# A five-stage layer on one Trainium2 core: the last image's scores on six banks, clears and queue instructions moved between engines

## The reference

```python
x = x + L0_conv_ref(gn(x))        # group norm, then a two-dimensional LSTM over rows and columns:
#   f0 = sigmoid(pf0 + h_up @ uf0), f1 = sigmoid(pf1 + h_left @ uf1), i, o, c~ from h_up + h_left
#   c = f0 * c_up + f1 * c_left + i * c~;  h = o * tanh(c)
t = tokens(x)                     # (16, 4096, 128)
t = t + L1_attn_ref(ln(t))        # Nystroem attention, 8 heads of 16, 64 landmarks:
#   q_l, k_l = means over 64 tokens
#   out = softmax(q k_l) @ pinv(softmax(q_l k_l)) @ (softmax(q_l k) @ v) + conv33(v)
t = t + L1_ffn_ref(ln(t))         # Wx = x W', batch-normalised; then 4096 steps in order:
#   y = sigmoid(Wx[:, t] + y @ V.T)
```

## Time and profile before

| | |
|---|---|
| median of 3 runs | 5966.88 us (5963.65 to 5968.33) |
| the profiled execution | 5969.65 us |
| its span | 5967.9 us |
| PE busy | 5291.5 us (89%) |
| ACT, DVE, POOL busy | 3264.5, 2989.0, 1673.9 us |
| mean granted clock of PE | 0.978 of 2.4 GHz |
| group norm / LSTM begins / landmark begins / recurrence begins | 0 / 221.4 / 1446.6 / 3660.3 us |

### The profile page before, as it was taken

The page is one execution under the profiler, slowest core; times in us unless marked ns, Lnnn a source line. Parts: engine busy times, 40 slices in busy tenths (PEclk is TensorE's granted clock), DMA queues, the critical chain, the costliest instruction groups (busy, mean ns, idle before and its releaser), DMA issues. The chain is left out here.

```text
span 5967.9 us, 208944 instructions
## 1 busy us (share of the span) xinstructions
PE 5291.5 (89%) x90032; PEld 3235.7 (54%) x90032; DVE 2989.0 (50%) x7682; ACT 3264.5 (55%) x9359; POOL 1673.9 (28%) x2017
## 2 busy tenths in 40 slices
PE   5599999997899997799999997888888888888888
PEld 4599888996566666644444443333333333333333
DVE  8677777775888885568888884000000000000000
ACT  5465555564677775479999994333333333333333
POOL 2100000002888874257877783000000000000000
PEclk7799999999999999999999998999999999999999
DMA  9631112225888772368777773111111111111111
GB/s 389 263 114 58 57 58 70 73 86 180 245 246 243 238 229 90 101 177 230 228 227 231 227 211 104 42 49 47 45 49 47 45 49 47 45 49 47 46 48 31
DMA packets 858992, 755.53 MB, mean 127 GB/s; under 512 B 71152, under 2 KB 732656, under 8 KB 854000
## 3 DMA queue, kind: packets, MB, share of 16 engines
q1 hardware_dynamic: 841120, 642.58, 36.1%
q0 software_dynamic: 14816, 99.32, 4.1%
q10 hardware_dynamic: 2160, 0.66, 0.0%
HBM read 425.72 MB, written 308.45 MB: 123 GB/s over the span
## 5 line engine op out<-in xcount | busy, mean ns | idle before, releaser
L2652 ACT ACTIVATE f_y<-f_acc 128x16 f32<-128x16 f32 x4096 | 753.7, 184 | 1544.0 <-PE f_acc L2618 1544.0
L2618 PEld LDWEIGHTS f_acc<-f_y,f_vT 128*32 128x32 f32 x32768 | 645.0, 108 | 1491.2 <-ACT f_y L2652 1491.2
L2618 PE MATMUL f_acc<-f_y,f_vT 128*32 128x16 f32 x32768 | 1045.8, 193 | 296.3 <-ACT f_y L2652 0.4
L2607 PE MATMUL f_junk<-f_idle 128*32 128x512 bf16 x12368 | 1226.0, 377 | 0.0
L2563 DVE TENSOR_TENSOR f_sum<-f_turned,f_t 128x512 f32<-128x512 f32 x128 | 88.5, 692 | 2072.3 <-PE f_turned L2600 2072.2
L2317 DVE TENSOR_REDUCE o_m<-o_bank_l 128x8 bf16<-128x512 f32 x512 | 327.3, 680 | 101.2 <-PE o_bank_l L2083 101.2
L2607 PEld LDWEIGHTS f_junk<-f_idle 128*32 128x32 bf16 x12368 | 368.0, 99 | 0.0
L1239 ACT ACTIVATE a_p<-a_s 128x512 f32<-128x512 f32 x512 | 264.2, 602 | 180.7 <-PE a_s L1111 180.6
L498 POOL DMA_DIRECT2D hidden<-l_h x46 | 34.6, 754 | 1160.2 <-DVE l_hsum L754 961.5
L677 ACT ACTIVATE l_gate<-l_pf,r_ctx 128x256 f32<-128x256 f32 (+7 forms) x512 | 202.4, 446 | 229.8 <-PE l_pf L608 229.7
L2268 ACT ACTIVATE o_p<-o_bank_s 128x512 f32<-128x512 f32 x512 | 264.4, 602 | 34.0 <-PE o_bank_s L2106 33.0
(11 more groups left out here) (274 smaller groups left out, 11174.4 us busy)
## 6 DMA issues: line engine op xcount, KB each, us to landing
o_v<-vals SPq DMA_DIRECT2D x256, 272.0 KB, 3.5
a_hid<-hidden SPq DMA_DIRECT2D x112, 520.0 KB, 5.1
hidden<-l_h POOLq DMA_DIRECT2D x46, 1040.0 KB, 6.7
l_x<-skew SPq DMA_DIRECT2D x46, 1024.0 KB, 5.2
vals<-a_v SPq DMA_DIRECT2D x128, 272.0 KB, 3.5
gn_x<-in_x SPq DMA_DIRECT2D x16, 2048.0 KB, 17.4
a_xin<-in_x SPq DMA_DIRECT2D x128, 256.0 KB, 4.9
tokens<-a_t SPq DMA_DIRECT2D x128, 256.0 KB, 3.4
```

The costliest lines, as they stand in the source:

```text
L2607: nc.tensor.matmul(junk[rows, :], idle[:, 0:QUAD], idle[:, :], start=True, stop=True)
L2618: mm = nc.tensor.matmul(acc[k % 2][rows, t, :], vT[:, rows], before, start=False, stop=True, skip_group_check=True)
L2652: nc.scalar.activation(y[q][:, u, :], acc[u // RC % 2][:, u % RC, :], ACT.Sigmoid).then_inc(s_y, 1)
```

## The change

1. The last store of the group norm is issued by ACT instead of POOL.
2. DVE's clear of `hw[1]` is two instructions; PE waits for the first (one of 8 windows' rows) alone.
3. The clear of `v[1]` goes from POOL (slot 4 of period 0) to DVE, in four parts in slots 3 to 6.
4. The rounded scores of image 15 are made one by one on the whole array, round the banks `L`, `proj`, `turn`, each waiting for the maximum three before it; those banks are read by `last_rounded_max`. The scores of image 14 no longer wait for maxima.
5. The exact scores of image 15 go round six banks (`S`, `proj`, `turn`), and may start when two of the four exponentials before them are done.
6. vT, gamma and beta of the recurrence are issued by ACT instead of SP.

```diff
--- before.py
+++ after.py
@@ -169,6 +169,6 @@
                 pool.tensor_tensor(rstd[:, :], veps[:, :], minus_half[:, :], ALU.pow).then_inc(s_pool, 1)
-                pool.wait_ge(s_vec, VS * (k + 1))
-                at = slice(0, ALONE) if s == 0 else slice(ALONE, STEPS * G)
-                done = S.late if k == NK - 1 else s_store[lane % DB]
-                pool.dma_start(skew[lane, :, at], D[lane % DB][:, at]).then_inc(done, 16)
+                if k < NK - 1:
+                    pool.wait_ge(s_vec, VS * (k + 1))
+                    at = slice(0, ALONE) if s == 0 else slice(ALONE, STEPS * G)
+                    pool.dma_start(skew[lane, :, at], D[lane % DB][:, at]).then_inc(s_store[lane % DB], 16)
             for q in range(DB):
@@ -225,2 +225,4 @@
                                    ).then_inc(s_copied, 1)
+            act.wait_ge(s_vec, VS * NK)
+            act.dma_start(skew[LANES - 1, :, ALONE:], D[LASTD][:, ALONE:]).then_inc(S.late, 16)

@@ -703,3 +705,4 @@
             nc.vector.memset(cell[:, :, :], 0.0).then_inc(s_begin, 1)
-            nc.vector.memset(hw[1][:, :, :, :], 0.0).then_inc(s_begin, 1)
+            nc.vector.memset(hw[1][:, :, WIN - 1, :], 0.0).then_inc(s_begin, 1)
+            nc.vector.memset(hw[1][:, :, 0:WIN - 1, :], 0.0)
             dve.wait_ge(s_begin, BEGIN)
@@ -849,2 +852,3 @@
         SET, CONST, SEL, CTX = 12, A.CONST, A.SEL, 3
+        QUARTERS = 4
         NL = PAIRS_H * NG
@@ -890,2 +894,13 @@
             return divmod(NG * p + c - k, NG)
+
+        def score_bank(i, c, g):
+
+            if i < B - 1:
+                return S[g][:, :]
+            return (S[0][:, :], S[1][:, :], S[2][:, :], S[3][:, :], proj[:, :],
+                    turn[:, :, :].rearrange("p k t -> p (k t)"))[(PAIRS_H * c + g) % 6]
+
+        def last_bank(j):
+
+            return (L[:, :], proj[:, :], turn[:, :, :].rearrange("p k t -> p (k t)"))[j % 3]

@@ -994,9 +1009,2 @@

-            def clear_second_values():
-                for c in range(CHAINS):
-                    for q in range(2):
-                        pool.wait_ge(s_st[c][q], 16 * (PAIRS - q))
-                pool.wait_ge(s_last, 16 * CHAINS)
-                pool.memset(v[1][:, :], 1.0).then_inc(s["const"], 1)
-
             def slot(p, c, q):
@@ -1006,3 +1014,2 @@
                     fill_halves()
-                    clear_second_values()
                 if valid(p - 1):
@@ -1089,2 +1096,16 @@

+            def last_rounded_scores(first, end):
+                i = B - 1
+                for j in range(first, end):
+                    if j % PAIRS_H == 0:
+                        wait(pe, "rk", NG * i + j // PAIRS_H + 1)
+                    if j == 0:
+                        wait(pe, "set", SET * i + 7)
+                        wait(pe, "valc", nth(i, NG - 1))
+                        wait(pe, "xnT", nth(i, NG - 1))
+                    wait(pe, "mx", NL * i + max(0, j - 2))
+                    g = j % PAIRS_H
+                    nc.tensor.matmul(last_bank(j), qbd_lp[:, P * g:P * g + P], k_lp[j // PAIRS_H % 3][:, :], start=True, stop=True
+                                     ).then_inc(s["lp"], 1)
+
             def turn_maxima(i):
@@ -1096,6 +1117,7 @@

-                wait(pe, "exp", PAIRS_H * (nth(i, c) - 1))
+                ahead = 2 if i == B - 1 and c else 0
+                wait(pe, "exp", PAIRS_H * (nth(i, c) - 1) - ahead)
                 if c == 0:
                     wait(pe, "set", SET * i + 9)
-                if i + 1 < B and c - 1 in SLOTS:
+                if i + 1 < B - 1 and c - 1 in SLOTS:

@@ -1104,3 +1126,3 @@
                     rows = slice(QUAD * g, QUAD * g + QUAD)
-                    nc.tensor.matmul(S[g][:, :], sel[rows, :], m3row[q][rows, :].unsqueeze(1).broadcast_to([QUAD, GT, P]),
+                    nc.tensor.matmul(score_bank(i, c, g), sel[rows, :], m3row[q][rows, :].unsqueeze(1).broadcast_to([QUAD, GT, P]),
                                      start=True, stop=False)
@@ -1110,3 +1132,3 @@
                         rows = slice(QUAD * g, QUAD * g + QUAD)
-                        ms = nc.tensor.matmul(S[g][:, P * k:P * k + P], kT[q][rows, at:at + P], qbd[q][rows, P * g:P * g + P],
+                        ms = nc.tensor.matmul(score_bank(i, c, g)[:, P * k:P * k + P], kT[q][rows, at:at + P], qbd[q][rows, P * g:P * g + P],
                                               start=False, stop=k == GT - 1)
@@ -1146,4 +1168,5 @@
                 j, e = before(p - 2, c)
-                maxima = valid(p - 1) and c in SLOTS
-                if maxima:
+                maxima = valid(p - 1) and p < B and c in SLOTS
+                last = p == B and c in SLOTS
+                if maxima or last:
                     first, four, end = spread(c)
@@ -1151,2 +1174,4 @@
                     scores(p - 2, c, q)
+                if last:
+                    last_rounded_scores(first, first + 2)
                 if c == 0 and valid(p - 2):
@@ -1175,2 +1200,4 @@
                     weigh(j, e, j % 2)
+                if last:
+                    last_rounded_scores(first + 2, end)
                 if valid(i):
@@ -1219,3 +1246,3 @@
                 if i == 1 and c == 0:
-                    act.wait_ge(s["const"], CONST + 2)
+                    act.wait_ge(s["const"], CONST + 1 + QUARTERS)
                 wait(act, "s", nth(i - 2, c))
@@ -1227,4 +1254,4 @@
                 wait(act, "vm", nth(i, c))
-                if i < 2 and c == 0:
-                    act.wait_ge(s["const"], CONST + 1 + i)
+                if i == 0 and c == 0:
+                    act.wait_ge(s["const"], CONST + 1)
                 wait(act, "pvd", nth(i - 2, c))
@@ -1238,3 +1265,3 @@
                 for g in range(PAIRS_H):
-                    nc.scalar.activation(p3[c % 2][g][:, :], S[g][:, :], ACT.Exp).then_inc(s["exp"], 1)
+                    nc.scalar.activation(p3[c % 2][g][:, :], score_bank(i, c, g), ACT.Exp).then_inc(s["exp"], 1)

@@ -1300,2 +1327,7 @@

+            def last_rounded_max(j):
+                c, g = j // PAIRS_H, j % PAIRS_H
+                wait(dve, "lp", NL * (B - 1) + j + 1)
+                nc.vector.tensor_reduce(m3p[:, g, c:c + 1], last_bank(j), AX.X, ALU.max).then_inc(s["mx"], 1)
+
             def after(i, k):
@@ -1341,2 +1373,12 @@

+            def clear_second_values(k):
+                if k == 0:
+                    for c in range(CHAINS):
+                        for q in range(2):
+                            dve.wait_ge(s_st[c][q], 16 * (PAIRS - q))
+                    dve.wait_ge(s_last, 16 * CHAINS)
+                    dve.wait_ge(s["const"], CONST + 1)
+                size = (NT * VROW + DH) // QUARTERS
+                nc.vector.memset(v[1][:, size * k:size * k + size], 1.0).then_inc(s["const"], 1)
+
             def row_sums(i):
@@ -1400,2 +1442,5 @@
                         rounded_max(p - 1, four - PAIRS_H + g, S[g])
+                if p == B and c in SLOTS:
+                    for j in range(*SLOTS[c]):
+                        last_rounded_max(j)
                 if c == NG - 1 and valid(p - 1):
@@ -1410,2 +1455,4 @@
                     landmark_maxima(p - 1)
+                if p == 0 and 3 <= c < 3 + QUARTERS:
+                    clear_second_values(c - 3)
                 if c == 0 and valid(p - 2):
@@ -2502,5 +2549,2 @@
                 load_wx(0, 0, g)
-            for dst, src in ((vT[:, :], ffn_v_t), (gam[:, :], gamma.rearrange("(p a) -> p a", a=1)),
-                             (bet[:, :], beta.rearrange("(p a) -> p a", a=1))):
-                sp.dma_start(dst, src).then_inc(s_w, 16)
             for g in range(GR):
@@ -2643,2 +2687,5 @@
         def _(act):
+            for dst, src in ((vT[:, :], ffn_v_t), (gam[:, :], gamma.rearrange("(p a) -> p a", a=1)),
+                             (bet[:, :], beta.rearrange("(p a) -> p a", a=1))):
+                act.dma_start(dst, src).then_inc(s_w, 16)
             act.wait_ge(s_const, 4)
```

## The result

The changed kernel takes **5933.75 us** (median of 5 runs, 5929.61 to 5939.81), the kernel before beside it 5966.88. The ratio is 0.9949, with a 95% interval of 0.9938 to 0.9961: 33 us less, or 0.5%. The forecast was 5933, in a range from 5923 to 5947, and faster by over 0.2% with a chance of 0.93. The profiled execution has a span of 5932.0 us, 35.9 less than that of before.

What follows compares the result with a forecast made beforehand. The recurrence's 4096 dependent steps stay; waits at four places bound the rest. Gains of 3.5 + 5.4 + 18.6 + 5.5 + 1.1 = 34.1 us take 5969.65 to 5935.5; the median, 2.8 lower, gives 5933, range 5923 to 5947.

Steps and rivals of the forecast that it cites:

- LSTM clear: LSTM start: splitting DVE's clear of the state gains 0, since the loads cover it.
- Clear of the second values: Landmark period 0: moving the clear from POOL to DVE gains 5.4 us; ends 3.7 and 5.8.
- Period 16: Landmark, slot 2 to the next period's slot 0: 25.9 us for 44.5, a gain of 18.6 us.
- Period 17: Landmark: slots of 2.55 us for 3.49, column sums adding 0.95; a gain of 5.5 us.
- The clock does not fall: Period 16: PE busy 3.6 of 4.1 us, so full clock taken; the rival, clock falls again, 5945, chance 0.14.
- The rival's: Periods 16 and 17: PE at 1.2 GHz for half, about 12 us of 24 lost, 5945 us; chance 0.14.
- Recurrence: Recurrence start: small loads on ACT's queue bring the first normalisation 1.1 us earlier; ends 0 and 2.6.
- The slower rival: Period 16: rounded score and maximum strictly in turn, 1.17 us each at full clock; kernel 5991 us, chance 0.03.
- the five terms: Store on ACT's queue 3.5, second-values clear 5.4, period 16 18.6, period 17 5.5, recurrence's small loads 1.1; sum 34.1 us.
- Turns of one packet: LSTM start: store rows and load packets go one for one, so PE starts 3.5 us earlier; the skill page's rule gives sum 36.

Runs made afterwards that it cites:

- the store alone: Kernel before, with only the last lane's store moved to ACT's queue; ratio 0.9995 (0.9986 to 1.0004), normalising's end to PE 15.49 us, before 18.28.
- the run with the ones only: Changed kernel with ACT's late store issued after the first two LSTM loads, and DVE's second-values clear cut to pieces of 256 and 16 elements; 5932.40 us.
- the kernel with the loads first: Changed kernel, with ACT issuing the late store inside the LSTM block once the first two loads landed; 5920.11 us, ratio 0.9933 to the kernel before.
- the run that was to vary the amount in flight: Changed kernel, late store of 32 of its 128 rows, an earlier SP store filling the other 96; load's first packet 1.05 us after issue.

## Why the prediction was right, point by point

- **LSTM clear: 0.** Shown by the store alone.
- **Clear of the second values: 4.1 us for 5.4.** The forecast took "four slots after 1472.69 it begins at 1498.14, where 4 x 4.9 would give 1492.3". The last two of these slots are not 4.9 us long even without the clear on POOL: from the seventh addition to the eighth are 5.3 us, and from the eighth to the next period's first 6.3. With the clear on POOL they are 10.4 and 5.2. The addition behind the clear is 5.1 us earlier (36.5 for 41.7), and 1.0 of it is absorbed at the border of the period. The step that failed is the yardstick of 4.9 us a slot across a border: four slots without the clear take 21.4 us, not 19.6.
- **Period 16: 17.5 us for 18.6.** The sum of 25.9 came out at 27.0, 0.2 to 0.4 us too long in each of slots 2, 3, 4 and 7. One thing makes up the difference: the third rounded score stands behind 1.1 us of weighing in PE's queue, so DVE idles 0.36 us before the third maximum. Moving it takes 0.38, 0.37, 0.20 and 0.37 us from these four slots and gives 25.7, more than the difference. I had counted DVE's work and the hand-overs, and had not gone through PE's order between the second and the third score, though it stands in the code. The 44.5 us are one draw of the old stretch; the three other kernels with four banks had 43.4, 43.9 and 45.0.
- **Period 17: 5.4 us for 5.5.** This hit is luck in part: both ends of the subtraction were too low. The sum had 18.9 us for the seven intervals and 19.5 came; it had 24.4 for the old ones and they took 24.9, the first two of them 3.80 and 3.67 us with a piece at 1.2 GHz. Five of the new intervals are 2.50 to 2.74 for 2.55, the fourth is 3.03 and the one with the column sums 3.47, for 3.5; in two other traces of the same code the seven sum to 18.8.
- **The clock does not fall: right.** The granted clock is 1.00 in both stretches. Of the 14 traces, the four with four banks and the one with a single bank have 1.2 GHz somewhere in period 16, the nine with two or three banks nowhere. The old stretch's 0.73 was part of its 44.5 us: a slot there takes 6.55 us at full clock and 6.8 to 7.8 with a piece at 1.2 GHz, so at least 1.4 of the 17.5 us are the clock's, from slots 2 and 3 (7.58 and 6.91). The rival's "half of periods 16 and 17, as it was before" holds for period 16 alone: 23.9 of its 44.5 us were at 1.2 GHz, and 3.4 of the 24.9 in period 17.
- **Recurrence: 1.1 us for 1.1**, bound by the load of wx, as forecast. Between the two groups of traces it is 0.5 to 1.2 us; 1.1 is at the upper end.
- **The slower rival** was priced by its mechanism and not refuted by it: with one bank the price is real. The change has three, and the third is worth 3.3 us.

The total was nearer than its parts: 30.9 us by the five terms, and some 5 from stretches that the change doesn't touch, of which the pseudo-inverse and output stages scatter by 15 us from run to run. That the forecast hit 5933.75 to 1 us is partly luck. The five measured terms alone, taken from 5966.9, give 5936, within its own range of 5929 to 5939; that the untouched stretches didn't carry the result out of that range is luck again.

## What to carry to other kernels

A store left in flight over a stage border moves the border, not the work behind it: if the next stage begins with loads, issue these first and the store behind them. Here that hid the store's time as well. Where an engine has just enough idle time for a moved piece, the move is free, as the run with the ones only shows. Where several banks let two engines run past each other, count the banks by what stands in the writer's queue between two writes, and look for a write that needs no wait and can go ahead of the long work.

## What was not expected of the hardware

**A load issued into a busy queue starts late.** With no other transfer in flight, the first load's first packet moves 1.05 us after SP's issue begins (210.02 to 211.07, in the kernel with the loads first). With the store in flight it is 5.2 us with rows of 32 KB and 4.6 us with pieces of 2032 bytes. The other way round, the store issued into the running loads begins 4.3 us after its issue (215.55 to 219.84). SP's own issues stretch with it, from 2.04 us for four to 9.80. The Trainium skill, page "DMA: Bandwidth & Descriptors", section "Latency and other measured facts", has about 0.6 us to the first byte of a hardware queue. The idle case agrees with it, if the 0.39 us of the issue itself are taken off 1.05; the busy case is seven to eight times that. What holds the start is not settled: it hardly depends on the row size, and in the run that was to vary the amount in flight, the store was over before the loads came.

**Turns of one packet.** The same page of the Trainium skill, section "Queues, rings and completion order", has an engine drain a packet of some 9 to 17 descriptors before it changes queues. In the changed kernel from 214.4 to 218.9 the 16 engines moved 63 packets of each queue, four on each engine, and in every microsecond about as many of the one as of the other; no turn of 9 is to be seen. By that rule, as an estimate from that page of the Trainium skill, the loads would have been through in 4 to 7 turns, among 8 rows of the store. The measurement disagrees, and the sum was made by it.

**The clock in periods 1 and 2.** From the first addition of period 1 to that of period 3 the 14 traces have the same work and take 102.2 to 107.2 us. The five with 3.4 us at 1.2 GHz in it take 102.2 to 103.1, the two with 6.8 us 103.5 and 104.1, and the seven with 10 to 17 us 104.9 to 107.2. A straight line through them has 0.32 us lost for each at the lower clock (correlation 0.89). This is a correlation; no run changes the clock alone. PE was busy 79 of 102 us in the kernel with the loads first, and 83 of 107 in the changed one. In period 0, the two kernels with the full clear on POOL have 20 us at 1.2 GHz, all others about 13. So a wait that was taken from POOL here also gave back clock next to it. But what the clock does further on differs from run to run by as much as such a term: the changed kernel's two periods are 4.6 us longer than those of the kernel with the loads first, with the same instructions.
